# Group weights applied to the SiLU and to the up sum in the middle of a quad, instead of to the finished products

## Chip, cores and metric

One core of one Trainium2 chip. The metric is the device time of one execution in microseconds; several runs of each kernel are timed and the median counts.

## What is computed

Tokens (8 x 256 of width 512) pass through a cross attention with a residual, then through a routed feed-forward layer with a residual. The change lies in the second part. For a token n and each of 8 groups g of 352 inner rows:

```python
g = einsum('ngh,gih->ngi', xg, gate_proj_w)
u = einsum('ngh,gih->ngi', xg, up_proj_w)
a = silu(g) * u
d = einsum('ngi,ghi->ngh', a, down_proj_w)
y = einsum('ng,ngh->nh', scalar, d)
```

`xg` is the normalized token plus a small product of its routing shares with `mask_up_w`. `scalar[n, g]` is the sum of the token's chosen expert weights in group g. The kernel brings it ahead of the down product: it multiplies `a` by `scalar` (times the gain of the residual), so that the down products of all groups can be summed in one bank.

## The kernel before

The kernel is written by hand, engine by engine: each engine has a list of instructions in a fixed order, and semaphores join them. Nothing is planned by a tool; the place of a call in a list is its place in the engine's queue.

**Quads.** The feed-forward layer runs in 2 passes of 1024 tokens. A pass has 11 units of 256 inner rows; a unit is two quads (j = 0, 1) of 128 inner rows, 44 in all. `quad.p` is the unit within the pass: `quad.p == 0` holds for quads 0, 1, 22 and 23. A quad forms gate and up sums for two chunks of 512 tokens. Instead of eight block products it makes seven, in the manner of Strassen and Winograd, each of 6 matmuls (three terms of a split into high and low fp32r halves, over two k tiles), and four soft products for the mask-up part. VectorE and ACT combine the banks in `tmp[quad.set]`, a tile with four slots: SUM_1, SUM_2, SUM_3 and ACTED. Two such tiles alternate between even and odd quads.

**TensorE's order in a quad** from 3 on: products 1 and 6; in the first pass masked products (8 short matmuls, L1743) for the mask-up factors; in some quads a small routing matmul, ahead of which TensorE waits for all residual sums of the quads before (`ROUTED_ON_ODD`); products 2, 5, 7; two soft products (L1735); two early down products; products 4 and 3 with a soft product each; two late down products. Quads 0 to 2 and 43 have no early ones. A down product (L85, 6 matmuls) writes bank 6 or 7 in turn, so each waits until VectorE has added the one before the last to the residual (`s_res`). The down products run one unit behind.

**VectorE's order in a quad**: the second sum (L1395); in the first pass the a_stack chain (`a_tile`: L1356, L1359, L1365, L1367), for which the soft products wait; the third sum (L1434) and C22 (L1441), which leaves the up sum of the second chunk in SUM_3; early residual sums (`add_down`, L1383); routing steps or a piece of token sums in some quads of the first pass; C21 (L1487), the up sum of the first chunk, in SUM_1; the first product (L1492), ACTED times SUM_1; its scale (L1376); C12 (L1499), the gate sum of the second chunk, in SUM_2; residual sums; the second product (L1402), SUM_3 times SUM_2; its scale (L1376 again). In quad 2 one residual sum stands between first product and scale, one after the scale. Quads 0 and 1 make their second product in the next quad.

**ACT**: the first sum's copy (L961), the casts of the next quad's weights (L825), the first SiLU (L1022) into ACTED, the second SiLU (L1044) in place in SUM_2, and casts of both finished activations to their high half (`act_high`, L930), for which `s_act` is waited. In odd quads the cast of the first activation stands before the second SiLU, in even ones behind it. `down_weights` (L944) casts the down weights in even quads, behind the cast of the previous quad's second activation.

**POOL** forms low halves: of the activations (`act_low`, L723), the down weights (L718) and the weights (L672), and weight sums (L661 to L666); in quads 12, 14, 16 and 18 token sums as well.

`s_prod` counts finished products, `s_act` finished scaled activations. The group weights come by DMA into `scalars` before quad 0 and again before quads 22 and 23; only there (`quad.p == 0`) does the scale wait for them.

```python
dve.wait_ge(s_silu_0, q + 1)
nc.vector.tensor_tensor(sums[:, ACTED], sums[:, ACTED], sums[:, SUM_1], ALU.mult).then_inc(s_prod, 1)
if q == 2:
    add_down(below)
scaled(quad, 0, sums[:, ACTED])
if q == 2:
    add_down(below + 1)
```

Of the kernel before, what the change touches and what calls it, by code (L numbers as in the profile page):

```python
# [5 lines left out]
ALU = mybir.AluOpType  # L6
# [17 lines left out]
HALF_G = G // 2  # L24
# [18 lines left out]
SUM_1, SUM_2, SUM_3, ACTED = range(4)  # L43
# [85 lines left out]
def layer_program(nc, x, ctx_nat, ctx_t, w_qkvo, w_gate_up, w_down, mask_up, gate_t, inv_map, gains, out):  # L129
    with ExitStack() as stack:  # L130
        def sem(name):
            return stack.enter_context(nc.semaphore(name))

        def width(shape):
            n = 4
            for extent in shape[1:]:
                n *= extent
            return (n + 31) // 32 * 32
# [123 lines left out]
        def piece_home(i):  # L262
# [14 lines left out]
        tmp = [nc.alloc_sbuf_tensor_at(f"tmp_{i}", [P, 4, BANK], F32, offset=at_scores + i * width([P, 4, BANK]))  # L277
               for i in range(2)]
# [14 lines left out]
        scalars = nc.alloc_sbuf_tensor_at("scalars", [P, 2, 2, BANK], F32, offset=at_ot)  # L293
# [21 lines left out]
        def at_block(u, j, c):  # L315
# [54 lines left out]
        s_scal_in = [sem(f"scal_in{j}") for j in range(2)]  # L370
# [8 lines left out]
            sem, ("m1_ready", "m6_ready", "m2_ready", "m5_ready", "c11_ready", "m7_ready", "m4_ready", "m3_ready"))  # L379
        s_s1, s_s2, s_s3, s_c22, s_c21, s_c12 = map(  # L380
            sem, ("sum1_done", "sum2_done", "sum3_done", "c22_done", "c21_done", "c12_done"))
        s_silu_0, s_silu_1, s_prod, s_act = map(sem, ("silu0_done", "silu1_done", "prod_done", "act_ready"))
        s_at_hi, s_at_lo = sem("at_hi_done"), sem("at_lo_done")
        s_down, s_res = sem("down_ready"), sem("residual_done")
        s_out = sem("out_stored")
# [24 lines left out]
        def _(sp):  # L410
# [56 lines left out]
            def store_piece(i):  # L467
                _, _, at = piece_tokens(i)
                sp.wait_ge(s_piece_lo, i + 1)
                for dram, part in ((th_dram, sums_hi), (tl_dram, sums_lo)):  # L470
                    sp.dma_start(dram[:, :, :, at:at + PIECE].rearrange("p t k n -> p (t k) n"),
                                 f32(part[piece_home(i)][:]).rearrange("p c k n -> p (c k) n")).then_inc(s_piece_out, 16)
# [287 lines left out]
        def _(eng):  # L760
# [195 lines left out]
            def first_sum(quad):  # L956
                q = quad.q
                eng.wait_ge(s_m1, q + 1)
                if q >= 2:
                    eng.wait_ge(s_prod, 2 * q - 3)  # L960
                nc.scalar.copy(tmp[quad.set][:, SUM_1], bank[BANKS[quad.set][0]][:]).then_inc(s_s1, 1)  # L961

            for quad in quads:
                q, u, s = quad.q, quad.u, quad.s
                sums = tmp[quad.set]
# [3 lines left out]
                if q != 1:  # L969
                    first_sum(quad)  # L970
# [57 lines left out]
                if q == 0:  # L1028
                    first_sum(after)
# [21 lines left out]
        def _(dve):  # L1051
# [315 lines left out]
                nc.vector.tensor_tensor(a_stack[A_LO, j], scratch[A_LO], f32(a_stack[A_LO, j]),  # L1367
                                        ALU.subtract).then_inc(s_a_st, 1)

            def scaled(quad, c, part):  # L1370

                q = quad.q
                dve.wait_ge(s_prod, 2 * q + c + 1)
                if quad.p == 0:
                    dve.wait_ge(s_scal_in[quad.j], 16 * HALF_G * (quad.s + 1))
                nc.vector.tensor_tensor(part, part, scalars[:, quad.j, c], ALU.mult).then_inc(s_act, 1)  # L1376

            def add_down(n):

                u, t = divmod(n, UNIT_TILES)  # L1380
                row = xres[:, u // PAIRS * UNIT_TILES + t, :]
                dve.wait_ge(s_down, n + 1)
                nc.vector.tensor_tensor(row, row, bank[6 + t % 2][:], ALU.add).then_inc(s_res, 1)  # L1383
# [6 lines left out]
            def second_sum(quad):  # L1390
                q = quad.q
                sums = tmp[quad.set]
                dve.wait_ge(s_s1, q + 1)
                dve.wait_ge(s_m6, q + 1)
                nc.vector.tensor_tensor(sums[:, SUM_2], sums[:, SUM_1], bank[BANKS[quad.set][1]][:],  # L1395
                                        ALU.add).then_inc(s_s2, 1)

            def second_activations(quad):
                sums = tmp[quad.set]
                dve.wait_ge(s_silu_1, quad.q + 1)  # L1400
                dve.wait_ge(s_c22, quad.q + 1)
                nc.vector.tensor_tensor(sums[:, SUM_3], sums[:, SUM_3], sums[:, SUM_2], ALU.mult).then_inc(s_prod, 1)  # L1402
                scaled(quad, 1, sums[:, SUM_3])

            for quad in quads:
                q = quad.q
                sums = tmp[quad.set]
# [37 lines left out]
                if q == 1:  # L1445
                    second_activations(quads[0])
                    late_x2_lo(B - 1, 6)
                if q == 2:
                    second_activations(quads[1])
                    route_centre(B - 2, 7)  # L1450
                for n in range(early):
                    add_down(below + n)


                if q == 3:
# [31 lines left out]
                nc.vector.tensor_tensor(sums[:, SUM_1], sums[:, SUM_1], psum_b[:], ALU.add).then_inc(s_c21, 1)  # L1487
                if q == 0:
                    second_sum(quads[1])
                dve.wait_ge(s_c21, q + 1)  # L1490
                dve.wait_ge(s_silu_0, q + 1)
                nc.vector.tensor_tensor(sums[:, ACTED], sums[:, ACTED], sums[:, SUM_1], ALU.mult).then_inc(s_prod, 1)  # L1492
                if q == 2:
                    add_down(below)
                scaled(quad, 0, sums[:, ACTED])
                if q == 2:
                    add_down(below + 1)
                dve.wait_ge(s_m3, q + 1)
                nc.vector.tensor_tensor(sums[:, SUM_2], sums[:, SUM_2], psum_c[:], ALU.add).then_inc(s_c12, 1)  # L1499
# [5 lines left out]
                if q == 1:  # L1505
                    second_sum(quads[2])
                    a_tile(quads[2])
                elif q >= 2:
                    second_activations(quad)
# [11 lines left out]
        def _(pe):  # L1521
# [291 lines left out]
            def soft_products(quad):  # L1813
                q, s, j = quad.q, quad.s, quad.j
                psum_a, _, psum_c = banks_of(quad)
                if s == 0:
                    pe.wait_ge(s_a_st, q + 1)
                else:
                    pe.wait_ge(s_a_in[j], 16 * (quad.p + 1))
                if quad.p == 0:  # L1820
                    pe.wait_ge(s_soft_in[j], 16 * (s + 1))
                soft_product(psum_c, quad, UP, 1).then_inc(s_m5, 1)
                soft_product(psum_a, quad, GATE, 0).then_inc(s_c11, 1)
# [168 lines left out]
```

## Time and profile before

| | |
|---|---|
| median of 3 runs | 1057.75 us (1057.2 to 1058.01) |
| the profiled execution | 1059.39 us, span of its instructions 1057.6 us |
| TensorE busy | 1047.7 us (99%), weight loads 894.7 us (85%) |
| VectorE busy | 748.4 us (71%) |
| ACT busy | 390.9 us (37%) |
| POOL busy | 616.6 us (58%) |
| DMA | 111.66 MB, mean 106 GB/s |

The attention part ends near 304 us, where quad 0 begins; quads 0 to 21 run until about 688 us, quads 22 to 43 until 1038, and down products close the kernel. Busy times are unions of instructions on an engine. A row of a timeline gives the start in us from the span's start, the duration in us, engine, line, operation, tiles, shapes and the count of merged instructions; brackets hold the engine's idle time before it and what ended it.

### The profile page before, as it was taken

To read this page: it belongs to the slowest core of one execution; us is meant where nothing else is said; L and a number is where in the kernel's file an instruction comes from. 1 tells how busy PE (TensorE), PEld (TensorE's weight loads), DVE (VectorE), ACT (ScalarE), POOL (GpSimd) and SP (SyncE) were. 2 spreads that over 40 slices of the span, in tenths; PEclk is the share of its full clock that TensorE was granted. 3 is DMA by queue.
4 is the path that set the end of the run, shared out by engine and by line. 5 is a ranking of instruction groups with operands and counts; after the bars stand their busy time and mean duration, and the time that the engine had idled before them with its cause. 6 is when DMAs were issued, how large, how long until landed. Compare 5 with 4: busy or idle time off the path is not lost.

```text
span 1057.6 us, 14596 instructions
## 1 busy us (share of the span) xinstructions
PE 1047.7 (99%) x5428; PEld 894.7 (85%) x5428; DVE 748.4 (71%) x1315; ACT 390.9 (37%) x651; POOL 616.6 (58%) x546
## 2 busy tenths in 40 slices
PE   9999999999999999999999999999999999999998
PEld 9989989998988788878888878888888888888887
DVE  7874655676678788788789998766566566565565
ACT  5333324334434434243335333333333333332331
POOL 2012102122435976768788978768777677677661
PEclk9999999999999999999999999999999999999999
DMA  9212225255786315124223552683321220221202
GB/s 324 86 41 100 61 50 150 65 130 147 239 245 210 116 36 55 68 77 36 91 86 111 86 137 92 216 257 115 115 75 48 76 74 29 75 75 48 75 27 80
DMA packets 114341, 111.66 MB, mean 106 GB/s; under 512 B 20960, under 2 KB 96736, under 8 KB 114272
## 3 DMA queue, kind: packets, MB, share of 16 engines
q1 hardware_dynamic: 113840, 110.58, 35.9%
q8 instruction: 43, 0.70, 0.3%
q14 instruction: 26, 0.21, 0.1%
q10 hardware_dynamic: 432, 0.17, 0.1%
HBM read 79.07 MB, written 31.65 MB: 105 GB/s over the span
## 4 chain that ended last, share of the span: by engine, by line
PE 89%; DVE 7%; DMA 1%; issue 1%; SPq 1%; ACT 0%; POOL 0%; DVEq 0%; POOLq 0%
PE bank L85 37%; PE bank L1729 33%; PE bank L1540 9%; PE bank L1735 3%; PE bank L1559 2%; PE bank L1743 2%; DMA x2t<-x2l 1%; DVE tmp L1376 1%; DVE a_stack L1367 1%; PE bank L1714 1%; PE bank L1611 1%; DVE a_stack L1365 1%; DVE a_tmp L1359 1%; SPq L484 1%; DVE tmp L1402 1%
## 5 line engine op out<-in xcount | busy, mean ns | idle before, releaser
L1729 PE MATMUL bank<-x2t,wgu_hi 128*128 128x512 f32 x1144 | 353.0, 390 | 0.0
L672 POOL TENSOR_TENSOR wgu_lo<-wgu_raw,wgu_hi 128x768 fp32r<-128x768 f32 (+2 forms) x143 | 221.8, 1558 | 87.2 <-ACT wgu_hi L825 84.7
L1729 PEld LDWEIGHTS bank<-x2t,wgu_hi 128*128 128x128 f32 x1144 | 214.9, 188 | 44.3
L1729 PE MATMUL bank<-x2t,wgu_lo 128*128 128x512 f32 x572 | 224.2, 392 | 1.2 <-DVE tmp L1434 0.8
L825 ACT CAST wgu_hi<-wgu_raw 128x512 fp32r<-128x512 f32 (+1 forms) x129 | 93.8, 728 | 223.5 <-PE bank L1735 186.2
L1383 DVE TENSOR_TENSOR xres<-xres,bank 128x512 f32<-128x512 f32 x175 | 119.6, 683 | 47.7 <-PE bank L85 47.2
L85 PE MATMUL bank<-wd_hi,at_second 128*128 128x512 f32 x336 | 130.8, 389 | 0.0
L1729 PEld LDWEIGHTS bank<-x2t,wgu_lo 128*128 128x128 f32 x572 | 107.4, 188 | 24.4 <-issue 2.4
L644 POOL TENSOR_TENSOR kt_lo<-ctxt_raw,kt_hi 128x256 fp32r<-128x256 f32 x32 | 23.4, 762 | 136.8 <-ACT kt_hi L833 136.8
L85 PE MATMUL bank<-wd_hi,at_first 128*128 128x512 f32 x256 | 99.8, 390 | 0.4 <-DVE xres L1383 0.4
L1376 DVE TENSOR_TENSOR tmp<-tmp,scalars 128x512 f32<-128x512 f32 x88 | 89.6, 1018 | 4.4 <-DMA scalars<-scals 1.4
L718 POOL TENSOR_TENSOR wd_lo<-wd_raw,wd_hi 128x512 fp32r<-128x512 f32 x42 | 54.5, 1319 | 49.9 <-ACT wd_hi L944 49.9
L1434 DVE TENSOR_TENSOR tmp<-tmp,bank 128x512 f32<-128x512 f32 x44 | 30.2, 687 | 72.1 <-PE bank L1729 71.7
L85 PEld LDWEIGHTS bank<-wd_hi,at_second 128*128 128x128 f32 x336 | 63.1, 188 | 13.2
L1540 PE MATMUL bank<-xnt_hi,w_hi_qkv 128*128 128x256 f32 x256 | 71.9, 285 | 0.0
L1540 PE MATMUL bank<-xnt_hi,w_lo_qkv 128*128 128x256 f32 x256 | 71.7, 285 | 0.0
L1540 PE MATMUL bank<-xnt_lo,w_hi_qkv 128*128 128x256 f32 x256 | 67.6, 283 | 0.0
L85 PE MATMUL bank<-wd_lo,at_second 128*128 128x512 f32 x168 | 65.4, 389 | 0.0
L1022 ACT ACTIVATE tmp<-bank 128x512 f32<-128x512 f32 x44 | 26.4, 600 | 105.4 <-PE bank L1735 102.8
L1735 PE MATMUL bank<-soft_t,a_stack 128*128 128x512 f32 x176 | 62.3, 395 | 2.1 <-DVE a_stack L1367 2.0
L723 POOL TENSOR_TENSOR at_second<-tmp,at_second 128x512 fp32r<-128x512 f32 x44 | 59.0, 1341 | 8.3 <-ACT at_second L930 8.3
L723 POOL TENSOR_TENSOR at_first<-tmp,at_first 128x512 fp32r<-128x512 f32 x33 | 46.1, 1401 | 24.8 <-ACT at_first L930 24.8
(222 smaller groups left out, 2270.0 us busy)
## 6 DMA issues: line engine op xcount, KB each, us to landing
wgu_raw<-in_w_gate_up SPq DMA_DIRECT2D x43, 512.0 KB, 4.1
wd_raw<-in_w_down SPq DMA_DIRECT2D x22, 512.0 KB, 5.1
a_stacks<-a_stack SPq DMA_DIRECT2D x22, 192.0 KB, 1.9
a_stack<-a_stacks SPq DMA_DIRECT2D x22, 192.0 KB, 3.9
ctxt_raw<-in_ctx_t SPq DMA_DIRECT2D x8, 512.0 KB, 11.4
ctx_raw<-in_ctx SPq DMA_DIRECT2D x8, 512.0 KB, 8.5
x<-x_raw SPq DMA_DIRECT2D x8, 512.0 KB, 7.8
sums_raw<-x SPq DMA_DIRECT2D x16, 256.0 KB, 3.6
```

Source lines behind the costliest of these rows:

```text
L85: last = nc.tensor.matmul(out, stationary, moving, start=n == 0, stop=n == len(pairs) - 1)
L672: last = nc.gpsimd.tensor_tensor(wgu_lo[:, part], raw_of(quad)[:, part], f32(wgu_hi[:, part]), ALU.subtract)
L718: nc.gpsimd.tensor_tensor(lo[:, j], wd_raw[:, j], f32(hi[:, j]), ALU.subtract).then_inc(s_wd_lo, 1)
L723: nc.gpsimd.tensor_tensor(lo, tmp[quad.set][:, SUM_3 if c else ACTED], f32(hi), ALU.subtract).then_inc(s_at_lo, 1)
L825: nc.scalar.copy(wgu_hi[:, group], raw_of(quad)[:, group]).then_inc(s_fw_hi, 1)
L1022: nc.scalar.activation(sums[:, ACTED], psum_a[:], ACT.Silu).then_inc(s_silu_0, 1)
L1376: nc.vector.tensor_tensor(part, part, scalars[:, quad.j, c], ALU.mult).then_inc(s_act, 1)
L1383: nc.vector.tensor_tensor(row, row, bank[6 + t % 2][:], ALU.add).then_inc(s_res, 1)
L1434: nc.vector.tensor_tensor(sums[:, SUM_3], sums[:, SUM_1], psum_b[:], ALU.add).then_inc(s_s3, 1)
L1540: last = nc.tensor.matmul(bank[b0 + e // 2][:, (e % 2) * S:(e % 2 + 1) * S], stationary, moving, start=n == 0, stop=n == len(pairs) - 1)
L1729: last = nc.tensor.matmul(out_bank[:], stationary, moving, start=begins and n == 0, stop=n == len(pairs) - 1, skip_group_check=True)
L1735: return nc.tensor.matmul(out_bank[:], a_stack[:, quad.j, m, :], soft_t[:, quad.j, c, :], start=False, stop=True, skip_group_check=True)
```

## The change

The scales change operand and place. Instead of the finished products, the up sum of the second chunk (SUM_3) and the SiLU of the first chunk (ACTED) are multiplied by the group weights. In all quads but 0, 1, 22 and 23 both scales stand together behind the early residual sums, ahead of routing steps and C21; the first waits for C22, the second for the first SiLU. In those four quads the first scale stands between C21 and the first product, the other ahead of the second product. The products now count `s_act` themselves, `s_scaled` replaces `s_prod`, and ACT's copy of the first sum waits for `s_act`.

```diff
-        s_silu_0, s_silu_1, s_prod, s_act = map(sem, ("silu0_done", "silu1_done", "prod_done", "act_ready"))
+        s_silu_0, s_silu_1, s_scaled, s_act = map(sem, ("silu0_done", "silu1_done", "scaled_done", "act_ready"))
...
                 if q >= 2:
-                    eng.wait_ge(s_prod, 2 * q - 3)
+                    eng.wait_ge(s_act, 2 * q - 3)
...
-            def scaled(quad, c, part):
-
-                q = quad.q
-                dve.wait_ge(s_prod, 2 * q + c + 1)
+            def scale_second(quad):
+
+                q, up = quad.q, tmp[quad.set][:, SUM_3]
+                dve.wait_ge(s_c22, q + 1)
                 if quad.p == 0:
                     dve.wait_ge(s_scal_in[quad.j], 16 * HALF_G * (quad.s + 1))
-                nc.vector.tensor_tensor(part, part, scalars[:, quad.j, c], ALU.mult).then_inc(s_act, 1)
+                nc.vector.tensor_tensor(up, up, scalars[:, quad.j, 1], ALU.mult).then_inc(s_scaled, 1)
+
+            def scale_first(quad):
+
+                q, gate = quad.q, tmp[quad.set][:, ACTED]
+                dve.wait_ge(s_silu_0, q + 1)
+                if quad.p == 0:
+                    dve.wait_ge(s_scal_in[quad.j], 16 * HALF_G * (quad.s + 1))
+                nc.vector.tensor_tensor(gate, gate, scalars[:, quad.j, 0], ALU.mult).then_inc(s_scaled, 1)
...
             def second_activations(quad):
                 sums = tmp[quad.set]
+                if quad.p == 0:
+                    scale_second(quad)
                 dve.wait_ge(s_silu_1, quad.q + 1)
-                dve.wait_ge(s_c22, quad.q + 1)
-                nc.vector.tensor_tensor(sums[:, SUM_3], sums[:, SUM_3], sums[:, SUM_2], ALU.mult).then_inc(s_prod, 1)
-                scaled(quad, 1, sums[:, SUM_3])
+                dve.wait_ge(s_scaled, 2 * quad.q + 2)
+                nc.vector.tensor_tensor(sums[:, SUM_3], sums[:, SUM_3], sums[:, SUM_2], ALU.mult).then_inc(s_act, 1)
...
                 for n in range(early):
                     add_down(below + n)
+                if quad.p > 0:
+                    scale_second(quad)
+                    scale_first(quad)
...
+                if quad.p == 0:
+                    scale_first(quad)
                 dve.wait_ge(s_c21, q + 1)
-                dve.wait_ge(s_silu_0, q + 1)
-                nc.vector.tensor_tensor(sums[:, ACTED], sums[:, ACTED], sums[:, SUM_1], ALU.mult).then_inc(s_prod, 1)
+                dve.wait_ge(s_scaled, 2 * q + (1 if quad.p == 0 else 2))
+                nc.vector.tensor_tensor(sums[:, ACTED], sums[:, ACTED], sums[:, SUM_1], ALU.mult).then_inc(s_act, 1)
                 if q == 2:
                     add_down(below)
-                scaled(quad, 0, sums[:, ACTED])
-                if q == 2:
                     add_down(below + 1)
```

## Rows read from the trace of the kernel before

**Rows 1.** The page: its first line and TensorE's busy time.

```profile
span 1057.6 us, 14596 instructions
...
PE 1047.7 (99%) x5428; PEld 894.7 (85%) x5428; DVE 748.4 (71%) x1315; ACT 390.9 (37%) x651; POOL 616.6 (58%) x546
```

**Rows 2.** Stretches: length, busy us of PE, PEld, DVE, ACT, POOL, clock, DMA.

```profile
520.00:700.00 180.00, 178.65 (x826) 148.20 (x825) 153.84 (x191) 69.19 (x107) 150.47 (x121) 1.00 0.47 136
...
704.00:1034.00 330.00, 330.00 (x1451) 272.00 (x1449) 200.95 (x269) 113.08 (x185) 240.01 (x203) 1.00 0.21 70
```

**Rows 3.** TensorE's waits, 300 to 1058 us: us in total, times, longest.

```profile
PE bank L1735 <- DVE a_stack L1367: 2.0, 4, 1.3
PE bank L1624 <- DVE xres L1383: 1.2, 2, 0.6
PE bank L1729 <- DVE tmp L1434: 0.8, 2, 0.4
...
PE bank L85 <- DVE xres L1383: 0.4, 1, 0.4
PE bank L1601 <- DVE xres L1383: 0.3, 1, 0.3
PE bank L1618 <- DVE xres L1383: 0.3, 1, 0.3
```

**Rows 4.** Instructions on tmp: ns least/median/most, first and last start.

```profile
L1376 DVE TENSOR_TENSOR tmp<-tmp,scalars x88: 691/1111/1783, 331.8 to 1043.5; 128x512 f32<-128x512 f32 x88
```

**Rows 5.** Timeline of VectorE, quad 29 and the next quad's second sum.

```profile
815.45 0.69 DVE L1487 TENSOR_TENSOR tmp<-tmp,bank 128x512 f32<-128x512 f32 x1 [0.90 <-PE bank L1735]
...
817.06 1.12 DVE L1376 TENSOR_TENSOR tmp<-tmp,scalars 128x512 f32<-128x512 f32 x1
...
819.48 1.66 DVE L1402 TENSOR_TENSOR tmp<-tmp 128x512 f32<-128x512 f32 x1
...
822.61 0.69 DVE L1395 TENSOR_TENSOR tmp<-tmp,bank 128x512 f32<-128x512 f32 x1 [0.75 <-PE bank L1729]
```

**Rows 6.** Timeline of POOL in the same stretch.

```profile
816.56 1.07 POOL L666 TENSOR_TENSOR wgu_raw<-wgu_raw 128x256 f32<-128x256 f32 x1
...
819.31 1.28 POOL L723 TENSOR_TENSOR at_second<-tmp,at_second 128x512 fp32r<-128x512 f32 x1
```

**Rows 7.** Timeline of VectorE in quad 2.

```profile
355.12 0.68 DVE L1487 TENSOR_TENSOR tmp<-tmp,bank 128x512 f32<-128x512 f32 x1
...
356.55 0.69 DVE L1383 TENSOR_TENSOR xres<-xres,bank 128x512 f32<-128x512 f32 x1
```

**Rows 8.** Timeline of POOL in quad 2.

```profile
354.09 3.05 POOL L672 TENSOR_TENSOR wgu_lo<-wgu_raw,wgu_hi 128x256 fp32r<-128x256 f32 x3
357.09 1.29 POOL L723 TENSOR_TENSOR at_second<-tmp,at_second 128x512 fp32r<-128x512 f32 x1
```

**Rows 9.** Timeline of TensorE in quad 2: first matmuls of the third and fourth down products.

```profile
357.70 0.39 PE L85 MATMUL bank<-wd_hi,at_first 128*128 128x512 f32 x1
...
358.84 0.39 PE L85 MATMUL bank<-wd_hi,at_second 128*128 128x512 f32 x1
359.58 0.50 PE L85 MATMUL bank<-wd_hi,at_first 128*128 128x512 f32 x1 [0.36 <-DVE xres L1383]
```

**Rows 10.** Timeline of TensorE, the routing matmul of quad 5.

```profile
401.34 0.41 PE L1624 MATMUL bank<-ident,rest 128*64 128x128 f32 x2 [0.60 <-DVE xres L1383]
```

**Rows 11.** Timeline of VectorE, the two scales of quad 4.

```profile
395.33 1.67 DVE L1376 TENSOR_TENSOR tmp<-tmp,scalars 128x512 f32<-128x512 f32 x1
...
399.03 1.66 DVE L1376 TENSOR_TENSOR tmp<-tmp,scalars 128x512 f32<-128x512 f32 x1
```

**Rows 12.** Timeline of ACT, the first copy of quad 5.

```profile
398.68 0.58 ACT L961 COPY tmp<-bank 128x512 f32<-128x512 f32 x1
```

**Rows 13.** Timeline of TensorE, quad 6: last product matmuls, then the soft products.

```profile
422.56 0.61 PE L1729 MATMUL bank<-x2t,wgu_hi 128*128 128x512 f32 x2
423.25 0.73 PE L1735 MATMUL bank<-soft_t,a_stack 128*128 128x512 f32 x2
```

## The prediction

> **What bounds the kernel now.** I read the page first: TensorE is busy for 1047.7 us of a span of 1057.6 [rows 1]. Then its busy time by stretches: all 330 us from 704 to 1034 us (nearly the whole second pass) and 178.65 of 180 from 520 to 700, at a granted clock of 1.00, the 2.4 GHz level, while VectorE has 201 and 154 us of work there [rows 2]. So an edit on VectorE can only win what TensorE loses in waits, or make new ones. TensorE's list of waits after 300 us shows how little there is: 4.2 us put down to VectorE's a_stack and residual sums (2.0 + 1.2 + 0.4 + 0.3 + 0.3), and 0.8 to the sum at L1434 where no down product stands in between [rows 3]. All else that the edit touches is hidden behind matmuls; the question is how far each delayed step is from its matmul.
>
> **What one scale costs.** The 88 scales at L1376 take 0.69 us at least, 1.11 at the median, 1.78 at most [rows 4]. The spread is a collision with POOL. In quad 29 the scale at 817.06 takes 1.12 behind POOL's 256-column operation that ends at 817.63, and the second product, issued at 819.48 just after POOL's subtraction at 819.31, takes 1.66: it ends 0.55 us after that one's end [rows 5, 6]. So an operation with two SBUF inputs waits for POOL's running instruction, and POOL for it. Where POOL runs its chain of 256-column sums, or subtracts weights, I take 1.1 per scale; the bounds are 0.69 and 1.67.
>
> **The change, part by part.** The counts stay: two scales and two products a quad, no DMA added or removed, the semaphore of finished products replaced by one of finished scales. What moves is order.
>
> *Ordinary quads of the second pass (24 to 42): 0 us.* Two scales now stand between the early residual sums and the sum at L1487. That sum had 0.90 us idle before it [rows 5]; the scales take 2.2, so it comes 1.3 late. The first product follows without its scale (1.12 off) but may meet POOL's 512-column subtraction (0.5 to 0.6 more). In quad 29 that gives: L1487 at 816.8, product until 818.75, L1499 0.65 late, the SiLU and the cast of the first product with it; the second product again meets POOL's subtraction of that cast and ends at 821.8. Today the last scale ends near 821.85: its 0.7 us are gone and the delay has eaten them. The next quad's L1395 at 822.61 waits 0.75 us for TensorE [rows 5], so nothing reaches it. If that cover were gone, the seventh product would start late. The first scale's new wait on the first SiLU holds nothing: that SiLU needs one ACT operation after the soft products, the scale stands behind two down products. ACT's L961 and SP's loads of scalars wait for finished activations of a quad or more before. No queue but VectorE's is passed.
>
> *Quad 2: +1.5 us.* Here there is no cover. L1487 starts at 355.12 with no idle before it [rows 7]. The two scales of quad 2 come before it, while POOL subtracts weights (354.09, 3.05 us for three) [rows 8]: +2.2. The first residual sum, which ended at 357.24 [rows 7], ends at 359.4. TensorE's third down product waits for it and began at 357.70 unhindered [rows 9]: it begins 1.75 late. Today the fourth waits for the second sum: it starts at 359.58 where 359.07 was possible (0.23 after the matmul before), 0.51 [rows 9]. That goes, since no scale stands between the two sums any more. Net +1.24; if the product meets the subtraction that POOL starts at 357.09 [rows 8], 0.5 more. I take 1.5. Bounds: +0.4 with scales of 0.69, +2.8 with 1.67 and the collision.
>
> *Quads 5 and 9: -1.0 us together.* Their routing matmuls wait for the last residual sum of the quad before: 401.34 with 0.60 put down to it, quad 9 alike (1.2 in two) [rows 3, 10]. In quad 4 the scales take 1.67 and 1.66 [rows 11]; moved among POOL's 256-column sums 1.1 each, and a product may lose 0.6 to POOL: VectorE comes free 0.5 to 1.1 earlier. But L1499 comes up to 1.2 later, and behind it on ACT stand the second SiLU, the cast of the first product and the next quad's first copy, which starts at 398.68 today [rows 12] and would end near 400.8; the second product could start at 400.7. ACT's queue is late next, so I take 0.5 from each. Bounds 0 and -1.5.
>
> *Even quads 4 to 20: +0.4 us together.* There the a_stack chain on VectorE runs through POOL's low halves of the down weights, which start after ACT has cast the previous quad's second activation. So its end follows that activation's: in quad 6 the soft product starts at 423.25, 0.24 late [rows 13]. By the working for quad 29 an odd quad loses what it saves; with routing or piece work before L1487 the product arrives later against POOL, up to 0.6 more. Of nine even quads I count five with nothing to spare and four with 0.2 us. I take +0.4 in all; bounds -1.5 and +3.0. The longest wait, 1.3 [rows 3], stays: its chain begins on TensorE's masked products, not late.
>
> *Quad 43: +0.2 us.* It has no early down products. The sum at L1499 comes about 0.25 late, as POOL's last down weights run beside the scales; the residual sum behind it is just in time for the third down product today. Bounds 0 and +0.6. The end, 16 us of down products, is unchanged.
>
> *Quads 0, 1, 22, 23: 0.* The order changes by one place; in quad 22 the wait for the scalars now holds the product and L1499 0.7 us longer, under TensorE's lead.
>
> Sum: 1.5 - 1.0 + 0.4 + 0.2 = **+1.1 us**. The profiled execution took 1059.39 us (span 1057.6 and 1.8 around it), 1.6 above the median of the runs, 1057.75. It would become 1060.5, and the median **1058.8**.
>
> A rule can be weighed here. The rows say 1.1 for a scale among short POOL operations. The Trainium skill's page "SBUF — State Buffer", section "SBUF: two separate sides", says that VectorE and GpSimd share a port pair under an exclusive lock, and the loser waits for the winner's whole instruction. If both scales of quad 2 came just behind a winner, they would cost the upper bound of 1.67 each and the sum by that rule would be +2.0, an estimate of 1059.7.
>
> **Rivals.** *Faster: VectorE comes free early at the quads' ends.* If the scales fill idle time ahead of L1487 and POOL stays out of the way, TensorE's waits on VectorE go, all but the 1.3: 4.2 - 1.3 = 2.9; with quad 2 at +0.4 that is -2.5, **1055.2**. For it: 0.90 us idle in ordinary quads. Against: the waits stand behind quads whose L1487 has no idle, where moving saves nothing.
>
> *Slower: collisions with POOL in the first pass's odd quads.* Place: L1492 behind POOL's 512-column subtraction, then L1402 behind the activation's. Price: 0.4 us at each end; five even quads have no cover (5 x 0.4), four have half (4 x 0.2): +2.8 in place of +0.4, so **1061.2**. It decides from an average of 0.25 us per odd quad on. For it: the 1.66 of rows 5. Against: in quad 29 gain and loss cancel. By the lock rule named above such an arrival costs all of POOL's instruction, and the trace agrees with that 1.66.
>
> *The change does nothing*: every step lands in cover, quad 2 too; 1057.7, part of my "same".
>
> **How the numbers follow.** Forecast, with the null case, 0.50; faster rival 0.20; slower rival 0.30. A measurement of this kernel tells about 0.2% (2.1 us) from no change: the forecast lies within that, 1055.2 and 1061.2 outside. The range goes past both rivals' centres: 1055.0 to 1062.5.
>
> **What would show it.** Right: in quad 2 the third down product waits over a microsecond for a residual sum; 704 to 1034 us stays full; the routing waits in quads 5 and 9 shrink; scales keep a median near 1.1. Wrong: the a_stack waits gone or doubled, a wait of TensorE in the second pass, or ACT's first copy late enough to stop a second product.

## The result and the profile after

The changed kernel takes 1062.45 us in the median of 6 runs (1061.86 to 1065.11), the kernel before 1057.69 beside it; the ratio is 1.0046 [1.0036, 1.0056]. So it is slower by 4.8 us, more than the 0.2% that can be told from no change. The forecast was +1.1; 1062.45 lies 0.05 us inside the upper end of the range.

Three of the six runs (1061.86, 1061.87 and 1061.97) had a mean granted TensorE clock of 1.000, three (1062.93, 1064.09, 1065.11) had 0.998; the section on the hardware shows where the clock falls. At the full clock the loss is 1061.87 - 1057.69 = 4.2 us.

The page of the profiled execution (1061.86 us):

```profile
span 1060.1 us, 14596 instructions
...
PE 1047.7 (99%) x5428; PEld 894.8 (84%) x5428; DVE 752.8 (71%) x1315; ACT 386.5 (36%) x651; POOL 640.6 (60%) x546
```

TensorE has the same 1047.7 us of work as in [rows 1], so in this execution the whole loss is idle time of TensorE. VectorE's busy time grew by 4.4 us and POOL's by 24, with the same instruction counts: they hold each other up for longer. The stretches, columns as in [rows 2]:

```profile
520.00:700.00 180.00, 178.04 (x820) 147.06 (x819) 152.53 (x190) 66.83 (x107) 154.44 (x122) 1.00 0.45 131
704.00:1034.00 330.00, 329.47 (x1448) 271.57 (x1447) 202.95 (x270) 111.82 (x185) 256.19 (x204) 1.00 0.23 73
```

The second pass is full but for the wait for x2t at the pass change, which now falls inside the stretch. POOL is busy 16 us longer there than in [rows 2], and it costs nothing. The first pass has the loss. TensorE's waits from 300 us on, to be held against [rows 3]:

```profile
PE bank L1747 <- DVE a_stack L1367: 2.6, 8, 0.8
PE bank L85 <- DVE xres L1391: 2.1, 1, 2.1
...
PE bank L1630 <- DVE xres L1391: 0.8, 1, 0.8
PE bank L1613 <- DVE xres L1391: 0.8, 1, 0.8
PE bank L1741 <- DMA x2t<-x2l: 0.5, 1, 0.5
PE bank L1636 <- DVE xres L1391: 0.4, 2, 0.2
```

New are the 2.1 before a down product (quad 2), and eight waits for the a_stack chain in place of four. Such a row counts idle time from the modelled end of the matmul before, so a stop costs more than it shows: quad 6 has 0.20 here and lasts 0.50 longer. The routing waits in quads 4 and 8 (L1630, L1613) went from 0.3 each to 0.8, those in quads 5 and 9 (L1636) from 1.2 for both to 0.4. The scales, columns as in [rows 4], which has all 88 on one line:

```profile
L1384 DVE TENSOR_TENSOR tmp<-tmp,scalars x44: 684/1225/1781, 330.6 to 1038.5; 128x512 f32<-128x512 f32 x44
L1376 DVE TENSOR_TENSOR tmp<-tmp,scalars x44: 680/1159/1206, 337.8 to 1037.9; 128x512 f32<-128x512 f32 x44
```

**Quad 2.** Timeline of VectorE, then of TensorE:

```profile
354.63 0.70 DVE L1376 TENSOR_TENSOR tmp<-tmp,scalars 128x512 f32<-128x512 f32 x1
355.25 1.23 DVE L1384 TENSOR_TENSOR tmp<-tmp,scalars 128x512 f32<-128x512 f32 x1
356.40 0.68 DVE L1499 TENSOR_TENSOR tmp<-tmp,bank 128x512 f32<-128x512 f32 x1
357.11 1.74 DVE L1506 TENSOR_TENSOR tmp<-tmp 128x512 f32<-128x512 f32 x1
358.78 1.27 DVE L1391 TENSOR_TENSOR xres<-xres,bank 128x512 f32<-128x512 f32 x2
```

```profile
357.00 0.39 PE L85 MATMUL bank<-wd_hi,at_second 128*128 128x512 f32 x1
359.50 0.50 PE L85 MATMUL bank<-wd_hi,at_first 128*128 128x512 f32 x1 [2.11 <-DVE xres L1391]
```

The scales took 0.70 and 1.23, and the product 1.74 behind POOL's subtraction that starts at 357.04. The third down product starts 2.50 after the matmul before it, where 0.23 is the spacing without a wait: 2.27 lost. Before, the fourth lost 0.51 [rows 9], and has no wait now. Net: +1.8.

**Quad 5, an ordinary odd quad of the first pass.** To compare two traces I count from the start of the quad's last soft product on TensorE. Before it stood at 411.83, and these are the rows of TensorE, VectorE and POOL:

```profile
411.83 0.39 PE L1735 MATMUL bank<-soft_t,a_stack 128*128 128x512 f32 x1
...
411.33 0.67 DVE L1487 TENSOR_TENSOR tmp<-tmp,bank 128x512 f32<-128x512 f32 x1
412.04 0.69 DVE L1492 TENSOR_TENSOR tmp<-tmp 128x512 f32<-128x512 f32 x1
412.76 1.11 DVE L1376 TENSOR_TENSOR tmp<-tmp,scalars 128x512 f32<-128x512 f32 x1
...
416.87 0.69 DVE L1376 TENSOR_TENSOR tmp<-tmp,scalars 128x512 f32<-128x512 f32 x1
...
413.29 1.75 POOL L672 TENSOR_TENSOR wgu_lo<-wgu_raw,wgu_hi 128x512 fp32r<-128x512 f32 x1
```

And after, where it stands at 412.54, with TensorE's wait in quad 6:

```profile
412.54 0.39 PE L1747 MATMUL bank<-soft_t,a_stack 128*128 128x512 f32 x1
...
413.64 0.67 DVE L1499 TENSOR_TENSOR tmp<-tmp,bank 128x512 f32<-128x512 f32 x1
414.34 1.83 DVE L1506 TENSOR_TENSOR tmp<-tmp 128x512 f32<-128x512 f32 x1
...
417.47 1.28 DVE L1412 TENSOR_TENSOR tmp<-tmp 128x512 f32<-128x512 f32 x1
...
414.34 1.28 POOL L672 TENSOR_TENSOR wgu_lo<-wgu_raw,wgu_hi 128x512 fp32r<-128x512 f32 x1
...
424.43 0.73 PE L1747 MATMUL bank<-soft_t,a_stack 128*128 128x512 f32 x2 [0.20 <-DVE a_stack L1367]
```

C21 ended 0.17 after the soft product, now 1.77: the scales push it back by 1.6. The first product without its scale should give 1.1 of that back. It gives nothing: it is issued together with POOL's 512-column subtraction and takes 1.83, which is what product and scale took together (0.69 + 1.11, with a gap). The second activation was finished 5.73 after the soft product (416.87 + 0.69), now 6.21: 0.48 later. The next quad's second sum and a_stack chain stand right behind it, POOL's low halves of the down weights begin 0.48 later too, and quad 6 lasts 0.5 longer. The Trainium skill's page "SBUF — State Buffer", section "SBUF: two separate sides", has the loser of the shared port wait for the winner's whole instruction. By that rule the trace agrees: the product ends at 416.17, 0.55 after POOL's instruction.

Quad 29 shows why the second pass loses nothing (VectorE):

```profile
819.40 0.68 DVE L1499 TENSOR_TENSOR tmp<-tmp,bank 128x512 f32<-128x512 f32 x1
820.11 0.69 DVE L1506 TENSOR_TENSOR tmp<-tmp 128x512 f32<-128x512 f32 x1
...
822.10 1.11 DVE L1412 TENSOR_TENSOR tmp<-tmp 128x512 f32<-128x512 f32 x1
```

With 0.90 us of idle to fill, C21 is 1.2 late (by the same way of counting; this trace runs 2.70 behind that of before there), the product meets no subtraction, and the second activation is finished 1.35 earlier than before.

### The profile page after: what moved, and what is told of

It is laid out like the page before. It is cut to its first block, busy times and chain, and to the rows that moved or that the text cites. A ratio compares the mean times of both kernels' runs of the same rounds, so it can differ in the third digit from the quotient of the medians.

```text
span 1060.1 us, 14596 instructions
## 1 busy us (share of the span) xinstructions
PE 1047.7 (99%) x5428; PEld 894.8 (84%) x5428; DVE 752.8 (71%) x1315; ACT 386.5 (36%) x651; POOL 640.6 (60%) x546
## 4 chain that ended last, share of the span: by engine, by line
PE 85%; DVE 9%; issue 2%; DMA 1%; ACT 1%; SPq 1%; POOL 0%; DVEq 0%; POOLq 0%
PE bank L85 36%; PE bank L1741 31%; PE bank L1552 9%; PE bank L1747 3%; PE bank L1571 2%; DMA x2t<-x2l 1%; PE bank L1755 1%; DVE a_stack L1367 1%; DVE a_stack L1365 1%; DVE tmp L1506 1%; DVE tmp L1384 1%; DVE tmp L1376 1%; PE bank L1726 1%; DVE xres L1391 1%; SPq L484 1%
## 5 line engine op out<-in xcount | busy, mean ns | idle before, releaser
L672 POOL TENSOR_TENSOR wgu_lo<-wgu_raw,wgu_hi 128x768 fp32r<-128x768 f32 (+2 forms) x143 | 211.2, 1483 | 86.3 <-ACT wgu_hi L825 86.1
L1443 DVE TENSOR_TENSOR tmp<-tmp,bank 128x512 f32<-128x512 f32 x44 | 30.2, 687 | 71.4 <-PE bank L1741 71.2
L723 POOL TENSOR_TENSOR at_second<-tmp,at_second 128x512 fp32r<-128x512 f32 x44 | 64.3, 1462 | 13.9 <-ACT at_second L930 13.9
L1403 DVE TENSOR_TENSOR tmp<-tmp,bank 128x512 f32<-128x512 f32 x44 | 30.1, 685 | 55.9 <-PE bank L1741 54.5
L85 PEld LDWEIGHTS bank<-wd_hi,at_first 128*128 128x128 f32 x256 | 48.1, 188 | 12.8 <-DVE xres L1391 2.7
```

Source lines behind the costliest of these rows:

```text
L85: last = nc.tensor.matmul(out, stationary, moving, start=n == 0, stop=n == len(pairs) - 1)
L672: last = nc.gpsimd.tensor_tensor(wgu_lo[:, part], raw_of(quad)[:, part], f32(wgu_hi[:, part]), ALU.subtract)
L723: nc.gpsimd.tensor_tensor(lo, tmp[quad.set][:, SUM_3 if c else ACTED], f32(hi), ALU.subtract).then_inc(s_at_lo, 1)
L1443: nc.vector.tensor_tensor(sums[:, SUM_3], sums[:, SUM_1], psum_b[:], ALU.add).then_inc(s_s3, 1)
```

## The experiments

The kernels were run in three sets, each beside the kernel before: its medians were 1058.05 (27 runs), 1058.31 (33) and 1057.68 (29). Single executions of one kernel differ in places that no version touches: the attention part, the DMA wait at the pass change (quad 22), and a wait for the a_stack chain that makes quad 3 longer by 0.5 to 0.7 in some and is absent in others. So I also give a table by quads. It is worked out from each kernel's profiled execution: the length of a quad is the time from the last soft product's start in the quad before to its own. What stands is the difference to the second profile of the kernel before, in us; quad 3's length has the late down products of quad 2 in it. Each row is one execution, and that need not be a typical one: the profiled execution of the even quads alone took 1057.23, 1.6 above the median of its runs.

| kernel | median, ratio | quad 3 | 4, 8 | 6, 14, 18, 20 | 10, 12, 16 | 5, 9 | 17 | other 1 to 21 | 22 | 23 to end |
|---|---|---|---|---|---|---|---|---|---|---|
| before, first profile | | 0.66 | -0.01 | 0.08 | 0.05 | -0.01 | 0.07 | -0.01 | 0.11 | 0.07 |
| the change | 1.0046 | 1.83 | 0.87 | 2.30 | -0.06 | -0.84 | -0.39 | 0.13 | 0.26 | -0.13 |
| change again | 1.0043 | 3.48 | 0.86 | 2.29 | -0.09 | -0.84 | -0.35 | 0.11 | 1.72 | -0.11 |
| change but quad 2 | 1.0017 | 0.06 | 0.92 | 2.32 | -0.05 | -0.86 | -0.40 | 0.10 | -0.30 | -0.11 |
| quad 2 only | 1.0019 | 3.38 | 0.03 | 0.03 | -0.02 | -0.02 | 0.07 | -0.02 | -0.53 | 0.01 |
| quad 2 half | 0.9999 | 0.51 | -0.05 | 0.05 | 0.08 | 0.01 | 0.03 | -0.01 | -0.53 | 0.05 |
| odd quads only | 1.0020 | 0.05 | 0.99 | 2.30 | -0.05 | 0.01 | -0.51 | -0.03 | -0.53 | -0.01 |
| even quads only | 0.9975 | 0.05 | 0.06 | 0.07 | 0.13 | -0.88 | -1.51 | 0.06 | 1.29 | 0.08 |
| even and second pass | 0.9988 | 0.07 | 0.01 | 0.06 | 0.07 | -0.87 | -1.47 | 0.07 | -0.33 | -0.12 |
| before, short POOL | 0.9973 | 0.56 | -1.11 | 0.63 | 0.35 | -1.12 | -1.53 | 0.12 | -0.13 | 0.03 |
| odd, short POOL | 0.9991 | 0.53 | -0.19 | 0.12 | 0.09 | -1.15 | -0.36 | 0.15 | 0.08 | 0.08 |
| even, short POOL | 0.9988 | -0.02 | -1.11 | 0.64 | 0.38 | -1.61 | -1.25 | 1.24 | -0.23 | 0.03 |
| change, short POOL | 1.0018 | 3.43 | -0.24 | 0.07 | 0.13 | -1.61 | -0.28 | 1.22 | 0.34 | -0.12 |

The change's row adds to 3.97, against 4.2 by the medians at the full clock.

**Both kernels again.** No edit. The kernel before:

> The kernel before, unchanged, for a second profile. Its profiled execution took 1059.39 us where the median of its runs is 1057.7. If that profile was an unusual execution, this one has a span near 1055.9 and TensorE's idle time after 300 us, 8.7 us there, is about 1.7 us shorter here; then the changed kernel lost 4.2 us and not the 2.5 that the two spans show. If the profile was typical, the span is 1057.6 again and the 1.7 us lie outside the instructions. Both: ratio 1.000 within 0.001.

1057.76 us (11 runs), 0.9996 [0.9987, 1.0005]. Its span was 1055.7 against 1057.6 in the first profile: 0.84 less ahead of quad 1, 0.66 less in quad 3, 0.11 less at the pass change. The waits at the other places came back within 0.1 us.

> The changed kernel, unchanged, for a second profile and more runs. Theory B and rival C both: a mix of runs at 1.000 with about 1061.9 and at 0.998 with 1063 to 1065. TensorE's waits on the a_stack chain come again in the even quads 4, 6, 8, 14, 16, 18 and 20, each within 0.1 us of the first profile, if they follow from the order; if they differ by more, the collisions with POOL are chance.

1062.26 us (5 runs), 1.0043 [1.0031, 1.0056]. Every group of the table repeats within 0.04, but quad 3 (the clock, below) and quad 22 (the DMA wait, which is not the change's).

**Quad 2 apart from the rest.** A tuple names the quads whose scales stand in the middle, `LATE` those that have each scale ahead of its product; the others scale their finished products, as before. All kernels by quads are made so. In them ACT's copy of the first sum waits for a scaled activation in all quads, as in the changed kernel.

```diff
-                if quad.p > 0:
+                if q in MID:
                     scale_second(quad)
                     scale_first(quad)
...
+                if not (q in MID or q in LATE):
+                    scale_product(quad, 0, sums[:, ACTED])
```

The change with quad 2 as before (`MID`: all but 0, 1, 2, 22, 23; `LATE`: 0, 1, 22, 23):

> The change in all quads but quad 2, which keeps the scales on its finished products. Theory A (quad 2 costs what the scales ahead of its residual sum delay, some 1.7 us, and the rest of the loss is POOL collisions in the even quads of the first pass): 1062.45 falls to about 1060.2, and the third down product no longer waits. Theory B (beside that, TensorE's 2.3 us of waiting in quad 2 is what lets its clock fall in some executions, seen as a mean granted clock of 0.998 in three of six runs of the changed kernel): all runs at 1.000 and a median near 1059.9 with a spread below 1 us. Rival C (the clock falls whatever the wait): runs at 0.998 stay.

1059.79 us (11), 1.0017 [1.0008, 1.0026]. All eleven runs are at 1.000, as theory B had it, but they spread over 2.4 us and not over less than one. The kernel before with quad 2 alone changed (`MID = (2,)`, `LATE = ()`):

> The kernel before, with both scales moved in quad 2 alone. Theory A: +1.7 us, 1059.4. Theory B: as A in half of the runs, and 1 to 3 us more with a mean granted clock of 0.998 in the others. Rival C: no run at 0.998 more often than in the kernel before. Null case: +0, if what quad 2 loses is won back behind it (the changed kernel's wait in quad 3 is 0.5 us shorter): 1057.7 to 1058.2.

1059.76 us (11), 1.0019 [1.001, 1.0028]; two of the eleven runs are at 0.998, not half of them. By the medians the two parts cost 1.7 us each, 3.4 of the 4.2 that the change cost in the same set; by the ratios 1.8 and 2.0, 3.8 of 4.5. Quad 2 costs what was foreseen and a little more, and at least 1.7 us lie elsewhere.

Quad 2 with its first scale between C21 and the first product, the second ahead of the second product (`MID = ()`, `LATE = (2,)`):

> The kernel before; in quad 2 the first scale stands between the sum at C21 and the first product, the second one ahead of the second product, so only one scale comes before the residual sum. Theory B (the length of TensorE's wait decides whether its clock falls): the third down product waits for 0.9 to 1.4 us instead of 2.2, no run below 1.000, +0.5 to +1.0 us. Rival: a wait of that length already lets the clock fall in some runs.

1058.04 us (11), 0.9999 [0.9991, 1.0008]. TensorE's longest wait at the down products is 0.4, as in the kernel before; the scale took 0.81 and the product 1.05. I had expected a loss of 0.5 to 1.0 and there is none. So the price of quad 2 comes from both scales standing ahead of C21 and of the residual sum, and not from the operand that is scaled. The ratio shows no cost of ACT's new wait either.

**Even and odd quads of the first pass.** `MID` is 4, 6 ... 20, then 3, 5 ... 21, `LATE` is empty; quad 2 and the second pass are as before.

> The kernel before, with the scales moved in the even quads 4 to 20 alone. Theory A (moving pays in even quads, whose scales cost 1.67 and 1.66 behind POOL, and loses in odd ones): TensorE's waits in quads 5 and 9 fall from 0.76 to about 0.3 each, those in quads 4, 6, 8, 14, 16, 18 and 20 stay as before, and the time falls by 1.0 to 1.5 us. Rival D (the loss has nothing to do with odd or even; VectorE has the same work and only runs later): 0 to +1 us.

1055.66 us (11), 0.9975 [0.9966, 0.9984]: faster than both kernels, and by more than the 1.0 to 1.5 us that was expected.

> The kernel before, with the scales moved in the odd quads 3 to 21 alone. Theory A: the second activation of an odd quad is finished later, so POOL's low halves of the down weights start later in the next, even quad, and its a_stack chain with them: waits of 0.4 to 0.6 in quads 14, 16, 18 and 20 and 0.8 instead of 0.4 in front of the routing matmuls of quads 4 and 8, together +2.5 to +3.0 us. Rival D: half of that or less.

1060.69 us (11), 1.002 [1.0012, 1.0029], 2.4 us slower, just under what theory A had. TensorE's waits, first of the even, then of the odd version:

```profile
PE bank L1765 <- DMA x2t<-x2l: 1.5, 1, 1.5
...
PE bank L1771 <- DVE a_stack L1371: 0.5, 2, 0.3
...
PE bank L1660 <- DVE xres L1403: 0.3, 2, 0.2
```

```profile
PE bank L1771 <- DVE a_stack L1371: 2.4, 8, 0.7
PE bank L1660 <- DVE xres L1403: 1.2, 2, 0.6
PE bank L1654 <- DVE xres L1403: 0.9, 1, 0.9
...
PE bank L1637 <- DVE xres L1403: 0.8, 1, 0.8
```

The change has two opposite parts beside quad 2. Moving the scales in an odd quad makes the next even quad late: quads 4, 6, 8, 14, 18 and 20 each last 0.5 to 0.6 longer, 3.3 together, as in the full change (0.87 + 2.30 = 3.2). Moving them in an even quad takes 0.44 each from quads 5 and 9. It also takes away the longest wait of the kernel before, 1.3 in quad 17 [rows 3]. Rows of VectorE in that quad's chain, then of POOL, before, and then with the even quads moved:

```profile
609.42 1.41 DVE L1359 TENSOR_TENSOR a_tmp<-a_tmp 128x128 f32<-128x128 f32 x1
610.96 1.24 DVE L1365 CAST a_stack<-a_tmp 128x384 fp32r<-128x384 f32 x1
612.23 2.05 DVE L1367 TENSOR_TENSOR a_stack<-a_tmp,a_stack 32x384 fp32r<-32x384 f32 x1
...
609.37 2.61 POOL L723 TENSOR_TENSOR at_first<-tmp,at_first 128x512 fp32r<-128x512 f32 x2
611.94 1.94 POOL L672 TENSOR_TENSOR wgu_lo<-wgu_raw,wgu_hi 128x768 fp32r<-128x768 f32 x1
```

```profile
607.75 0.29 DVE L1363 TENSOR_TENSOR a_tmp<-a_tmp 128x128 f32<-128x128 f32 x1
608.17 1.25 DVE L1369 CAST a_stack<-a_tmp 128x384 fp32r<-128x384 f32 x1
609.45 1.52 DVE L1371 TENSOR_TENSOR a_stack<-a_tmp,a_stack 32x384 fp32r<-32x384 f32 x1
...
607.76 2.79 POOL L727 TENSOR_TENSOR at_first<-tmp,at_first 128x512 fp32r<-128x512 f32 x2
```

Before, POOL's subtractions of the activations begin at 609.37, just ahead of L1359, which takes 1.41, and the chain's last step falls on POOL's 768-column subtraction and takes 2.05. Without a scale at quad 16's end VectorE gets there just ahead of POOL (that row is L1363 there and starts at 607.75, POOL's at 607.76) and takes 0.29, and the last step is through before the 768-column subtraction: 1.1 and 0.5 us less in the two rows.

The parts don't add up. With the odd quads moved too, only 0.4 of this 1.5 is left. In the table, even and odd alone give -2.0 together at quad 17, and the change without quad 2 gives -0.4, 1.6 less. From quad 4 to 21 the change without quad 2 loses 2.0, where the two parts would add to 0.6, so quad 17 makes the whole difference.

**POOL's 512-column subtraction.** Each quad's last weight subtraction is split in two of 256 columns.

```diff
-... if quad.q in (2, 3) or quad.q == 1 and n < 2 else [group]
+... if quad.q in (2, 3) or quad.q == 1 and n < 2 or quad.q >= 4 and n == 2 else [group]
```

In the changed kernel:

> The change, with POOL's 512-column subtraction of the last weight group done as two of 256 columns in quads 4 to 43 (same work, two instructions). Theory L (VectorE's product at L1506 waits for the whole running POOL instruction: 1.76 to 1.84 us in quads 13, 17 and 19): those products take 1.3 at most, the even quads' a_stack waits shrink by 0.2 to 0.5 each, and the time falls by 1 to 2 us from 1062.3. Rival D: products unchanged or POOL later by its own extra instruction (some 0.1 us each); time 1062.3 or above.

1060.27 us (11), 1.0018 [1.0009, 1.0027], 2.0 to 2.2 us faster than the change's two medians, the upper end of what theory L had. In the odd version, in the kernel before as a control, and in the even version:

> Only the odd quads 3 to 21 scaled in the middle, and POOL's last 512-column weight subtraction of each quad from 4 on made as two of 256. With the odd quads alone the time was 1060.69. Theory (the first product of an odd quad stands behind POOL's 512-column subtraction for its whole length, 1.8 us where 1.3 is enough, and the delay runs through the second SiLU, ACT's and POOL's queues into the next even quad's a_stack): the first product takes 1.3 at most, the second activation ends half a microsecond earlier, and 1.3 to 2.3 us of TensorE's waits in even quads go: 1058.4 to 1059.4. Rival (what delays the odd quad is the order on VectorE alone, both scales ahead of C21, whatever POOL runs): the waits stay and the time is 1060.5 to 1061, a little more if the split subtraction costs POOL time.

> The kernel before with the split subtraction alone: the control for the two kernels that carry it. Theory: the split lengthens POOL's chain by 0.6 us a quad and shortens no collision that matters here, as the first product of an odd quad ends ahead of the subtraction: 1057.5 to 1058.3. Rival (the split is worth as much by itself as it was in the changed kernel, 2.2 us, and tells nothing of the change): 1055.5 to 1056.5.

> Even quads 4 to 20 scaled in the middle (1055.66 by itself) and the split subtraction. Theory (in this kernel only 0.5 us of a_stack waits and 0.7 of routing waits are left, and the odd quads' products don't meet the subtraction): no gain, 1055.3 to 1056.3. Rival (even quads too lose in collisions with the 512-column subtraction): 1054.6 or less. A third way: POOL's longer chain makes the low halves late and an a_stack wait comes back: 1056.5 or more.

They took 1056.85 us (11; 0.9991 [0.9983, 1.0]), 1054.83 (7; 0.9973 [0.9961, 0.9984]) and 1056.82 (11; 0.9988 [0.9979, 0.9997]). Only the last of the three fell where one of its sentences had put it, the third way's 1056.5 or more. The split brings 2.9 us to the kernel before, more than even the rival had for it, so the 2.2 that it brought to the change say nothing by themselves. With it the odd quads still cost 2.0 (1056.85 - 1054.83), where they cost 2.4 without. So, taken over the whole time, the collision explains little of what the odd quads cost.

The traces say where it holds. Quad 5 of the odd version with the split (TensorE, VectorE, POOL):

```profile
410.09 0.39 PE L1771 MATMUL bank<-soft_t,a_stack 128*128 128x512 f32 x1
...
411.92 1.27 DVE L1524 TENSOR_TENSOR tmp<-tmp 128x512 f32<-128x512 f32 x1
...
414.49 1.27 DVE L1425 TENSOR_TENSOR tmp<-tmp 128x512 f32<-128x512 f32 x1
...
411.90 1.89 POOL L676 TENSOR_TENSOR wgu_lo<-wgu_raw,wgu_hi 128x256 fp32r<-128x256 f32 x2
```

The product takes 1.27 instead of 1.83, and the second activation is finished 5.67 after the soft product, not 6.2. The loss of quads 6, 14, 18 and 20 falls from 2.30 to 0.12; against the control, 0.63, it is gone. In front of these four stand quads 5, 13, 17 and 19, the ones where the first product took 1.76 to 1.83. Their second activation was finished 0.5 to 0.6 later than in the kernel before; with the split in both it is finished 0.1 to 0.2 earlier than in the control. So there the collision is the cause, shown by its removal.

In quads 4 and 8 it is not: in front of them stand quads 3 and 7, where the product took 0.69 in the change. Their second activation is finished 0.4 to 0.5 later, without the split and with it, and 0.92 remains at quads 4 and 8 against the control (-0.19 to -1.11). The rows with the split account for it. In the middle the two scales of quad 3 take 1.16 and 1.23, both beside POOL's chain of sums; behind the products they took 1.11 and 0.69, the second with POOL out of the way. That is 0.59 more for the same work. No run takes this price apart from the order, so it is read from rows and not shown by a removal. And quad 17 costs 1.2 more than in the control, for the split had taken its wait away.

What the split does for the kernel before is to be seen in its trace: the first scale of quads 3, 4, 7 and 8 takes 1.11 instead of 1.67 [rows 11], the waits for the routing matmuls of quads 4, 5, 8 and 9, 1.8 in all, are gone, and so is quad 17's. Even version and split take largely the same waits, so together they win no more than one of them. In both kernels that have the split and the even quads moved, a new wait appears in quad 13 (0.9 to 1.0 of the 1.2 under "other"). There the a_stack chain's last step starts just behind POOL's 768-column subtraction (540.80 and 540.60 in the even version with the split) and takes 2.07 instead of 0.55: the collision that quad 17 had before.

**Second pass.** `MID` is 4, 6 ... 20 and 24 to 43.

> Even quads 4 to 20 and all quads of the second pass from 24 on scaled in the middle; odd quads of the first pass and quad 2 as before. Theory (as the prediction had it: in the second pass TensorE has no waits before or after, so the change costs and gives nothing there): within 0.5 of the even quads alone, 1055.2 to 1056.2, TensorE full from 704 to 1034 us. Rival (part of the loss of the changed kernel, 0.5 us or more, lies in the second pass: quad 43's third down product, or small stretches between matmuls): 1056.3 or more. The pass change's own DMA wait can move either number by a microsecond in one execution, so the medians decide.

1056.8 us (11), 0.9988 [0.9979, 0.9996]. By the median this is 1.1 above the even quads alone, or 1.4 by the ratios, as the rival had it. The trace doesn't bear it out: from quad 23 to the end it is 0.2 shorter (-0.12 against 0.08), as in the changed kernel, and each of the quads 24 to 42 lasts 15.93 us in both. This trace is of the fastest of its eleven runs (1054.91), that of the even quads alone of one of the slower ones. The two were run in different sets and their intervals overlap. Whether a difference is left, and where, stays open.

## Why the prediction was wrong

*What bounds the kernel*: right. But for some tenths at the pass change, the loss at the full clock is TensorE idle in the first pass, behind VectorE.

*One scale costs 1.1 beside POOL*: right, the medians are 1.16 and 1.23.

*Second pass, 0 us*: right by the trace (the medians of the last experiment leave it open), and quad 29's C21 came 1.2 late, where 1.3 was said. The product's collision was not there, so the activation is earlier and not even; the cover was not needed.

*Quad 2, +1.5*: right by mechanism and nearly by size, +1.8 in the trace, 1.7 by itself in the medians and 2.0 by the ratio. The scales took 0.70 and 1.23, and the collision of the product, which the step priced at half of its 0.5, came in full (1.74). The lower clock that can follow the wait stands in no step of the prediction.

*Quads 5 and 9, -1.0*: right, -0.84; the even version has the same -0.88.

*Even quads 4 to 20, +0.4*: **this is the step that failed**. They lose 0.87 + 2.30 - 0.06 = 3.1 us, beyond its upper bound of 3.0; the slower rival had +2.8 at this place, and in size it was the one that came true. That is luck in part: its collision was there in four of the six odd quads, and the quads behind 3 and 7 lost nearly as much without it. The step read "by the working for quad 29 an odd quad loses what it saves". But quad 29 has 0.90 idle ahead of C21 [rows 5], which swallows most of the two scales, and then an odd quad of the second pass even gains. In the first pass the same view shows 0.90 idle only at quads 11, 20 and 21, 0.2 to 0.3 at quads 6, 9, 12 and 18, and none at the others, 3, 5, 7, 13, 15, 17 and 19 among them, where routing or piece work fills it. There C21 is late by the scales or more: by 1.6 in quad 5, 2.3 in quads 13 to 19, 2.9 in quads 3 and 7. In four of these quads the product then falls on POOL's 512-column subtraction. The sentence names this, "up to 0.6 more", and then counts it as next to nothing. It should have been multiplied out: six even quads at 0.5 instead of nine at 0.05 in the mean. Only quad 12, behind quad 11, gained (0.3).

*The longest wait stays*: wrong in its reason. The wait of 0.20 for the masked products ahead of the chain hid that VectorE was itself late and colliding in quad 17. It fell by 0.4 in the change and by 1.5 with the even quads alone.

*Quad 43, +0.2*: the stretch from quad 23 to the end got 0.1 to 0.2 shorter. Small, with the wrong sign.

*Quads 0, 1, 22, 23, 0*: right for TensorE. In quad 22 the product waits 2.46 us for the scalars, where the scale waited 1.43, and C12 comes 1.0 late instead of 0.7; no wait of TensorE follows.

*The sum.* With 3.1 in place of 0.4, and -0.4 for quad 17, the prediction's own sum is 1.1 + 2.7 - 0.4 = 3.4. The table's 3.97 has small terms besides: +0.3 more in quad 2, +0.2 less won in quads 5 and 9, -0.3 for quad 43's term, +0.1 in the other quads, and +0.3 at the pass change, which is not the change's. The lower clock in half of the runs adds to the median. Of the signs named ahead, all those for "right" came, and one of those for "wrong": the a_stack waits doubled in number.

The chances were set too near to no change. The forecast's 0.50 rested on gains and losses cancelling in the odd quads, read from one quad of the other pass.

## What to carry to other kernels

A moved instruction's cost can't be read from one quad of a loop whose body differs: look for idle ahead of the new place in each kind of iteration, and multiply by their count. Two engines that hold each other up make a product's time depend on when it is issued; shortening the other engine's long instruction at that place may win where moving one's own loses (here 2.9 us won against 4.8 lost; the even quads alone win 2.6, and the two are too close to rank). And where a change has parts, run the parts, and then the whole: the even quads win 2.6 us, the odd ones lose 2.4, quad 2 loses 1.7, and together they lose 4.2 and not 1.5. Most of that difference, 1.6, is the even quads' best gain, which is lost again once the odd quads move; the rest was not traced, and single runs scatter by about a microsecond.

## What the runs showed of the hardware

One thing was not expected. In some executions TensorE runs at the lower clock after the long wait in quad 2. The rows are those of the changed kernel's second profile, TensorE's timeline and then a stretch (length, busy us of PE, PEld, DVE, ACT, POOL, clock, DMA):

```profile
359.02 0.50 PE L85 MATMUL bank<-wd_hi,at_first 128*128 128x512 f32 x1 [2.12 <-DVE xres L1391]
...
360.29 0.63 PE L85 MATMUL bank<-wd_hi,at_second 128*128 128x512 f32 x1
360.72 0.63 PE L85 MATMUL bank<-wd_hi,at_first 128*128 128x512 f32 x1
...
363.28 0.58 PE L1741 MATMUL bank<-x2t,wgu_lo 128*128 128x512 f32 x1
```

```profile
360.30:363.30 3.00, 3.00 (x9) 2.32 (x8) 1.34 (x2) 0.53 (x1) 3.00 (x5) 0.50 0.06 6
```

Eight matmuls start 0.43 us apart instead of 0.23 at a granted clock of 0.50, the 1.2 GHz level; in the trace this costs 1.6 us (3.48 - 1.83 in the table's column of quad 3, and 3.38 and 3.43 in two other kernels). The fall comes 1.2 us after the wait's end, with TensorE busy again. Four series of runs have this wait of 2.1 us (the change twice, quad 2 only, the change with short POOL pieces): of their 33 runs 12 have a mean clock of 0.998. All 184 other runs of the three sets, of kernels whose profiled execution waits there for 0.4 or less, had 1.000. Among them are profiled executions with a wait of 1.3 in quad 17 or of 1.5 at the pass change, and no lower clock behind either. What decides in which executions it falls stays open, and so does the whole price: within the four series, runs at 0.998 are slower than the others by 2.1, 0.9, 0.3 and 0.5 us in the mean, and single runs scatter by about a microsecond. The split subtraction's gain was the other surprise, told above.
